# LayerNorm of the next superchunk moved ahead of the gelus, its transposes ahead of the output projection, and four staging slots in the weight set-up

## What is computed

```python
xn = layernorm(x)                                   # no scale, no shift
q, k, v = xn @ wq.T + bq, xn @ wk.T + bk, xn @ wv.T + bv      # 16 heads of 64
intra = softmax(q @ k.T / 8) @ v                    # within each chunk of 128 tokens
inter = softmax(causal(q @ k_means.T / 8)) @ v_means # against the means of the chunks so far
attn  = (intra + inter) @ wo.T + bo
ffn   = gelu((xn @ U1) @ V1 + b1) @ U2 @ V2 + b2    # rank 256, 4096 hidden
out   = x + attn + ffn
```

## Time and profile before

| | us |
|---|---|
| median of the 2 runs shown | 3605.79 (3583.94 and 3627.64) |
| the profiled execution's own time | 3581.5 |
| its span, slowest core (core 0) | 3579.9 |
| spans of the 8 cores | 3568.1 to 3579.9 |
| mean granted TensorE clock of a core, share of full speed | 0.777 to 0.782 |
| TensorE matmul busy | 2419.0 (68%) |
| TensorE weight load busy (beside the matmuls) | 1137.8 (32%) |
| VectorE busy | 1055.8 (29%) |
| ScalarE busy | 1205.6 (34%) |
| POOL busy | 298.0 (8%) |

### The profile page before, as it was taken

How to read it: one execution, slowest core, us unless ns; L and a number is a source line. 1 busy time by engine, 2 the same in 40 slices (tenths; PEclk the granted TensorE clock), 3 DMA queues, 4 the chain that set the end, 5 groups by cost and what they waited for, 6 DMA issues and landing times.

```text
span 3579.9 us, 41017 instructions; the slowest of 8 cores (3568.1 to 3579.9 us)
## 1 busy us (share of the span) xinstructions
PE 2419.0 (68%) x14243; PEld 1137.8 (32%) x14403; DVE 1055.8 (29%) x2444; ACT 1205.6 (34%) x2080; POOL 298.0 (8%) x558
## 2 busy tenths in 40 slices
PE   1267857676875767767676785767767576785767
PEld 0224333232433323333332433323333332333333
DVE  2432241413224132231413214142231513224141
ACT  0025133241523325143242613325143242613333
POOL 1101010100101000010100101010010100101010
PEclk9986958778695876858677785876869688795878
DMA  7400101001010100101000010100101000010000
GB/s 117 85 1 3 47 3 47 2 13 36 3 48 3 48 1 7 42 2 48 2 19 30 3 47 3 47 2 2 48 2 48 2 19 30 2 48 3 24 2 25
DMA packets 45429, 86.05 MB, mean 24 GB/s; under 512 B 17292, under 2 KB 24108, under 8 KB 44972
## 3 DMA queue, kind: packets, MB, share of 16 engines
q1 hardware_dynamic: 18348, 67.24, 5.1%
q0 software_dynamic: 26880, 16.18, 3.3%
HBM read 62.03 MB, written 34.60 MB: 27 GB/s over the span
## 4 chain that ended last, share of the span: by engine, by line
PE 55%; DVE 19%; issue 8%; ACT 8%; DMA 2%; POOL 1%; DVEq 1%; ACTq 0%; POOLq 0%
PE B L435 13%; PE B L906 8%; PE B L454 6%; PE B L850 6%; PE B L874 6%; DVE kcol L484 4%; DVE z L560 4%; PE B L813 2%; DVE out_st L930 2%; DVE km_fm L489 2%; PE B L693 2%; ACT v_tm L354 2%; PE B L683 2%; PE B L757 2%; PE B L916 2%
## 5 line engine op out<-in xcount | busy, mean ns | idle before, releaser
L906 PE MATMUL B<-woT,attn_fm 128*128 128x512 bf16 x992 | 270.3, 417 | 292.1 <-DVE Q_fm L892 176.7
L858 ACT ACTIVATE H_rot<-B,b_f 128x512 bf16<-128x512 f32 x512 | 348.4, 687 | 92.0 <-PE B L850 91.8
L444 ACT ACTIVATE q_fm<-B,bq_eff 128x512 bf16<-128x512 f32 x128 | 88.0, 687 | 770.7 <-PE B L435 770.7
L874 PE MATMUL B<-H_rot,U 128*128 128x512 bf16 x1008 | 303.1, 384 | 17.5 <-ACT H_rot L858 15.6
L850 PE MATMUL B<-P_fm,V 128*128 128x512 bf16 x992 | 309.5, 399 | 6.2 <-issue 5.3
L626 PE MATMUL B<-identity,neglse 128*32 128x128 f32 x64 | 23.8, 372 | 400.9 <-DVE neglse L618 400.9
L435 PE MATMUL B<-xn_fm,wqT 128*128 128x512 bf16 x992 | 254.0, 417 | 55.4 <-DVE xn_fm L400 51.4
L468 DVE CAST v_tm<-B 128x512 bf16<-128x512 f32 x128 | 88.6, 692 | 679.4 <-PE B L462 679.4
L454 PE MATMUL B<-wvT,xn_fm 128*128 128x512 bf16 x1008 | 242.1, 380 | 0.8
L906 PEld LDWEIGHTS B<-woT,attn_fm 128*128 128x128 bf16 x1024 | 97.1, 103 | 437.1 <-issue 360.2
L556 ACT ACTIVATE B<-B,cvals 128x512 f32<-128x512 f32 x256 | 158.1, 657 | 219.5 <-PE B L545 219.5
(11 more groups left out here) (104 smaller groups left out, 3147.7 us busy)
## 6 DMA issues: line engine op xcount, KB each, us to landing
x_buf<-L_attn_hidden_states SPq DMA_DIRECT2D x16, 2048.0 KB, 9.5
out<-out_st SPq DMA_DIRECT2D x64, 512.0 KB, 2.7
V<-L_ffn_V POOLq DMA_DIRECT2D x1, 2048.0 KB, 24.9
U<-L_ffn_U POOLq DMA_DIRECT2D x1, 2048.0 KB, 42.0
H_rot<-L_attn_wq POOLq DMA_DIRECT2D x8, 256.0 KB, 3.9
H_rot<-L_attn_wk POOLq DMA_DIRECT2D x8, 256.0 KB, 3.8
H_rot<-L_attn_wv POOLq DMA_DIRECT2D x8, 256.0 KB, 3.9
H_rot<-L_attn_wo POOLq DMA_DIRECT2D x8, 256.0 KB, 4.1
```

What stands on the lines that cost most here:

```text
L858: pm.do("s", (lambda bk=bk, g=g: lambda e: e.activation(H_rot[:, (g % 4) * 512:(g % 4) * 512 + 512], B[bk][:], AF.Gelu_apprx_tanh, bias=b1 ...
L874: pm.do("t", (lambda gq=gq, rc=rc: lambda e: e.matmul(B[6 + rc][:], U2[:, gq * 256 + rc * 128:gq * 256 + rc * 128 + 128], H_rot[:, (gq % 4 ...
L906: e.matmul(B[bk][:], attn_fm[:, ec * 512 + st * 128: ec * 512 + st * 128 + 128], woT[:, ec * 1024 + half * 512: ec * 1024 + half * 512 + 512],
```

## The change

Three edits.

**Set-up.** There are four staging slots in place of two: the two halves of `H_rot` and the two halves of `A1T`, with a semaphore each; piece n uses slot n mod 4 and banks 2 x slot and 2 x slot + 1, so all eight banks are in use.

**LayerNorm tiles.** The four `emit_ln_tile` of superchunk `sc + 1` stand right behind the attention, ahead of the FFN loop.

**Transposes.** `emit_xnt` for superchunk `sc + 1` stands where the LayerNorm tiles stood: behind the FFN loop, ahead of the `Q_fm` copies and the output projection.

```diff
-    d_st = [Ctr(nc, "d_st0"), Ctr(nc, "d_st1")]
+    d_st = [Ctr(nc, "d_st0"), Ctr(nc, "d_st1"),
+            Ctr(nc, "d_st2"), Ctr(nc, "d_st3")]
...
-    stage = H_rot
+    stage_slots = [H_rot[:, 0:1024], H_rot[:, 1024:2048],
+                   A1T[:, 0:1024], A1T[:, 1024:2048]]
...
-            slot = (wi * 8 + fc) % 2
-            stg = stage[:, slot * 1024:(slot + 1) * 1024]
+            slot = (wi * 8 + fc) % 4
+            stg = stage_slots[slot]
...
         attn_done_v = c_v.n
         kq_guard = (c_t, c_t.n)
 
+        if sc + 1 < nsc:
+            ln_next = [emit_ln_tile(sc + 1, st, kq_guard) for st in range(4)]
+
...
         hflat_guard = (c_t, q_mm_done)
         if sc + 1 < nsc:
-            ln_next = [emit_ln_tile(sc + 1, st, kq_guard) for st in range(4)]
+            xn_ready_next = emit_xnt(ln_next)
...
         pq_guard = (c_t, c_t.n)
-        if sc + 1 < nsc:
-            xn_ready_next = emit_xnt(ln_next)
         attn_guard = (c_v, c_v.n)
```

## The result

The changed kernel takes 3484.56 us (median of 11 runs) against 3584.82 us for the kernel before (median of 10 runs on the same chips). The ratio is 0.9708, 95% interval 0.9678 to 0.9738: 2.9% faster; the medians lie 100 us apart. The profiled execution spans 3482.8 us on its slowest core, core 0, against 3579.9. The prediction was 3490 us with a range of 3448 to 3545.

The account below looks back on a forecast made before the run. TensorE was taken to stand still behind ScalarE and VectorE chains around the FFN and output projection, then restart at a lower clock. 15 superchunks at -3.7 us (-56) and set-up (-36) took 3581.5 to 3490 us, range 3448 to 3545.

Parts of the forecast that it names:

- LayerNorm ahead of the gelus, +7.8: At the FFN's start, gelu's table load comes later and TensorE waits for the first gelu: +7.8 us a superchunk.
- The extra for the clock: In the FFN behind the wait for the first gelu, TensorE restarts at its lower clock: +1.2 us, between 0 and 2.3.
- The table load in the attention, 0: At the next superchunk's first Exp, a 1.28 us table load hides inside ScalarE's wait for VectorE's sums: 0.
- The bound of 19 us: Upper end for the attention's table loads if ScalarE's wait did not cover them: 15 x 1.28 = 19 us.
- Transposes in front of `Q_fm`, -4.9: Ahead of the output projection, small matmuls and casts replace the LayerNorm chain: gap 6.7 us for 11.67, -4.9 a superchunk.
- The output projection's slow start, 0 between -2.3 and +0.5: The output projection still starts at the lower clock behind its gap: 0 us a superchunk, ends -2.3 and +0.5.
- the rival of 12%: The output projection starts fast because transposes break the standstill in two: 1.8 us more gained a superchunk, 3463 us; 12%.
- The step between superchunks, -5.8 and -2.0: The q projection directly follows the last bias matmul, -5.8 us, and keeps the upper clock, -2.0 us, a superchunk.
- the one window (1.3): Granted clock of 0.67 over 4 us at the q projection's start: a slow-start cost of 1.3 us.
- Set-up, -36: In weight loading, four slots hide the latency of pieces: 59.3 us against 95.3, -36 us, ends -21 and -46.
- I take 1.7: Set-up time per piece with four in flight, in us, chosen between 2.05 (DMA share) and 1.37 (VectorE's copies).
- The sum: Whole kernel: -56 us from 15 superchunks and -36 from the set-up, -92 on 3581.5, giving 3490 us.

Follow-up runs that it names:

- the experiment with 32 matmuls: The changed kernel with 32 more matmuls, read by nobody, ahead of the first U2 matmul in 15 superchunks: 3455.84 us, ratio 0.9652.
- ScalarE's help: The changed kernel with the second of each piece's two set-up copies on ScalarE, beside VectorE's first: 3486.19 us, ratio 0.9696.

## Why the prediction was right, step by step

**LayerNorm ahead of the gelus, +7.8.** +7.9. The duration of a tile without a table load, read between the loads of the earlier trace rows, and the start at the attention's last matmul were enough. The extra for the clock, put at 1.2 between 0 and 2.3, was 1.7 to 1.8, and the experiment with 32 matmuls shows that it is the clock. The number is inside its range partly by luck, for the reading under it was wrong. "The FFN pays about 1.8 behind 321.62 already" was read in superchunk 0, and is not so in most: on core 0 the kernel before starts the FFN at the upper level in 11 of 15 superchunks, and pays 0.4 us in the mean (27.1 against 26.7). The change did not add to a cost that was there; it brought the cost of one slow start, about 2 us, to the superchunks that had been free of it.

**The table load in the attention, 0.** There are 15 of them, and they shortened ScalarE's wait for VectorE by their own length. The bound of 19 us was not touched. The rule of the Trainium skill (ScalarE: Activation LUTs, What ACT_TABLE_LOAD costs) of a 1.38 us drain with each switch does not show: the load starts 0.02 us behind the last Exp and the gelu follows 0.01 us behind the load. Going by the page would have given 3511, and the measured 3485 lies with the rows.

**Transposes in front of `Q_fm`, -4.9.** -4.8 as read, about -5.1 without the missing record, by the sum as written: the casts' 5 us set the pace.

**The output projection's slow start, 0 between -2.3 and +0.5.** -0.8 as read, about -0.5 without the missing record. It stays, as the window with a clock of 0.50 shows. This is the term with the rival of 12%, and the rival fell.

**The step between superchunks, -5.8 and -2.0.** Both as predicted. The q matmul's mean (2.4) was nearer to the clock's price than the one window (1.3): that window lies in superchunk 1, whose q, k and v projection takes 46.3 us, while 9 of the 15 behind superchunk 0 take over 47.5 and one at the upper level throughout takes 44.9.

**Not foreseen: the attention, -0.3.** 5 us in all; its cause was not looked for and stays open.

**Set-up, -36.** -31.5, the one term that was clearly mis-sized. 1.4 us of it is an earlier start of the first piece (55.29 against 56.66), which is less than the cores of one execution differ (53.56 to 56.45 in the changed kernel); the loading itself gained 30.0 on core 0 and 31.7 in the mean of the eight cores. The step that was off is "I take 1.7" a piece: (65.3 - 4.2 - 2.4) / 31 = 1.9. The spacing of the first pair, 1.0 us, was a burst and no rate; the DMA share, which said 2.05, was nearer. The rule of the Trainium skill (DMA: Bandwidth & Descriptors, Anatomy of one DMA — SWDGE (gpsimd) path), 2.0 us plus the bytes at 436 GB/s, would have made VectorE's copies the bound; ScalarE's help changed nothing, and the engines moved 147 GB/s, counted as written, at a share of 1.00.

**The sum.** -92 predicted; -97 in the spans and -100 in the medians. The superchunks brought a little more, the set-up a little less.

**What the prediction did not ask.** It priced the LayerNorm's move and the transposes' move one by one, and each with the other in place. The sum was right, but it hides that the two overlap: either alone brings most of the gain. The prediction's own terms, set against a kernel with only one of the moves, would have given it beforehand: +5.0 - 5.8 - 2.0 = -2.8 a superchunk for the transposes alone, and +7.8 + 1.2 - 10.1 (the gap down to the two `Q_fm` casts) - 2.3 (no slow start) = -3.4 for the LayerNorm alone, against -3.7 for both.

## What to carry to other kernels

A chain on other engines that stands between two TensorE stages cost about its length here wherever it stood, unless it lay beside TensorE's work. Moved whole from the end of a stage to its start, the LayerNorm gave 12.5 us at one place and took 9.7 at the other. Cut into pieces that lie beside TensorE's work in several stages, it left a gap of 1.5 us in place of 11.7, at a price of 1.8 us for the transposes inside the FFN. After each move price the kernel with every part of the change left out once. And compare the last iteration with the one before it: what it lacks and how much shorter it is names a cost on the path, here eight VectorE instructions worth 94 us.

## What the runs showed of the hardware

- Filling a wait of TensorE with useless matmuls paid here only when little of the wait was left: 16 matmuls that left 4.3 to 6.1 us of standstill brought nothing, 32 that left 0.7 to 2.6 us brought 29 us of 3485 (20 by the ratios).
- With 32 matmuls, the standstills of 2.0 to 2.6 us (33 of 120) were followed by the lower level and those of 0.7 to 1.9 us (87) were not; the standstills of 8.6 to 9.5 us of the changed kernel were all followed by it. It is no rule for other places: in the kernel before 33 of 120 FFNs start at the lower level behind a standstill of 0.7 us.
- The clock can come up and fall again within one such wait: the 16 matmuls ran at 226 ns each at a granted clock of 1.00, the matmuls 5.5 us behind them at 0.50.
- Loads with a cast from f32 to bf16, 256 KB written each, come at one per 1.9 us with four in flight and one per 2.98 us with two; from issue to landing one took 5.5 us in the median with four in flight and 3.9 with two (core 0).
